# Decoder layer on one core: scores of two key tiles in a row, weighted sums two tiles at a time

## The reference

```
Q = split_heads(layernorm(x) @ Wq + bq)         # 4 batches, 16 heads, 256 queries, 8
K, V = split_heads(ctx @ Wk + bk), split_heads(ctx @ Wv + bv)   # 1601 keys
attn = softmax(Q @ K.T / sqrt(8))
x = x + merge_heads(attn @ V) @ Wo + bo
x = x + ffn(layernorm(x))
```

## Time and profile before

| | |
|---|---|
| median of 3 runs | 417.07 us (414.47 to 417.73) |
| the profiled execution's own time | 413.62 us |
| its span, first to last instruction | 411.8 us |
| busy: PE, DVE, ACT, POOL | 357.9, 306.6, 299.4, 131.6 us |
| mean granted clock of PE | 0.925 of full speed |

### The profile page before, as it was taken

How to read it: one execution, slowest core, us unless ns; L and a number is a source line. 1 busy time by engine, 2 the same in 40 slices (tenths; PEclk the granted TensorE clock), 3 DMA queues, 4 the chain that set the end, 5 groups by cost and what they waited for, 6 DMA issues and landing times.

```text
span 411.8 us, 11548 instructions
## 1 busy us (share of the span) xinstructions
PE 357.9 (87%) x4598; PEld 164.8 (40%) x4598; DVE 306.6 (74%) x692; ACT 299.4 (73%) x637; POOL 131.6 (32%) x205
## 2 busy tenths in 40 slices
PE   1645988989989989999898999998989999798946
PEld 0332333444534444444344444444334344353334
DVE  2373998779889988798788887998778899690022
ACT  1321226888979799889697898897697998969921
POOL 5721000379120206897200137992000036000010
PEclk9966555999999999999999999999899999999968
DMA  7063370003507312235160331343211420000000
GB/s 294 12 240 122 139 249 40 2 27 130 173 27 169 123 38 60 93 130 163 35 173 14 107 96 53 121 136 96 80 40 47 130 61 21 2 15 2 2 0 15
DMA packets 22203, 35.77 MB, mean 87 GB/s; under 512 B 1604, under 2 KB 19694, under 8 KB 22150
## 3 DMA queue, kind: packets, MB, share of 16 engines
q1 hardware_dynamic: 22150, 35.05, 26.8%
HBM read 19.25 MB, written 11.96 MB: 76 GB/s over the span
## 4 chain that ended last, share of the span: by engine, by line
PE 47%; DMA 13%; POOL 12%; ACT 11%; DVE 7%; issue 5%; SPq 4%; POOLq 0%; ACTq 0%; DVEq 0%
PE wsum L1013 16%; PE score L1027 10%; PE ring L983 8%; PE ring L1047 8%; DMA q_rows<-q_parts 5%; ACT probs L873 5%; POOL k_parts L547 4%; DMA k_rows<-k_parts 4%; POOL k_rest L584 3%; POOL k_parts L589 3%; DVE part_max L690 2%; DMA k_unit<-k_rows 2%; DMA q_unit<-consts 1%; SPq L435 1%; POOL xn L600 1%
## 5 line engine op out<-in xcount | busy, mean ns | idle before, releaser
L690 DVE TENSOR_REDUCE part_max<-ring 128x1 f32<-128x401 f32 x512 | 261.0, 568 | 43.8 <-PE ring L1047 42.8
L873 ACT ACTIVATE probs<-score 128x512 f32<-128x512 f32 (+1 forms) x416 | 223.1, 597 | 41.6 <-PE score L1027 38.1
L1047 PE MATMUL ring<-k_unit,q_unit 51*128 51x401 bf16 x512 | 143.2, 355 | 9.9 <-DMA q_unit<-consts 5.1
L1013 PE MATMUL wsum<-probs,v_unit 128*32 128x256 f32 (+1 forms) x1664 | 135.7, 394 | 2.0 <-ACT unit_ctx L878 2.0
L1027 PE MATMUL score<-q_unit,k_unit 51*128 51x256 bf16 (+1 forms) x832 | 123.9, 278 | 7.3 <-ACT probs L873 5.0
L1027 PEld LDWEIGHTS score<-q_unit,k_unit 51*128 51x128 bf16 (+1 forms) x832 | 47.2, 97 | 100.6 <-ACT probs L873 60.9
L1047 PEld LDWEIGHTS ring<-k_unit,q_unit 51*128 51x128 bf16 x512 | 47.3, 95 | 30.1 <-DVE part_max L690 10.8
L1013 PEld LDWEIGHTS wsum<-probs,v_unit 128*32 128x32 f32 (+1 forms) x1664 | 39.7, 109 | 41.3 <-issue 24.6
L547 POOL TENSOR_TENSOR max_parts<-neg_max,c_sb 128x8 bf16<-128x8 f32 x16 | 3.4, 210 | 150.8 <-DVE neg_max L694 150.7
L621 POOL TENSOR_SCALAR prob_norm<-prob_self,prob_rsum 128x128 f32<-128x128 f32 (+1 forms) x12 | 9.0, 766 | 43.1 <-DVE prob_rsum L766 43.1
L927 ACT ACTIVATE v_aug<-ring 128x128 f32<-128x128 f32 (+1 forms) x60 | 10.5, 261 | 16.1 <-PE ring L983 16.1
(11 more groups left out here) (111 smaller groups left out, 290.3 us busy)
## 6 DMA issues: line engine op xcount, KB each, us to landing
k_unit<-k_rows SPq DMA_DIRECT2D x32, 300.2 KB
v_unit<-v_aug SPq DMA_DIRECT2D x16, 234.0 KB, 5.9
ctx_sb<-ctx_t SPq DMA_DIRECT2D x4, 800.5 KB, 7.4
k_rows<-k_parts SPq DMA_DIRECT2D x4, 601.5 KB, 3.2
k_rows<-k_parts SPq DMA_DIRECT2D x4, 599.2 KB, 3.4
k_rows<-k_parts SPq DMA_DIRECT2D x4, 401.0 KB, 4.1
k_rows<-k_parts SPq DMA_DIRECT2D x4, 399.5 KB, 4.1
even<-ffn_rows SPq DMA_DIRECT2D x3, 512.0 KB, 3.8
```

Of the source, the lines that this page charges most:

```text
L690: v_.tensor_reduce(part_max[:, par, q, head, hp, c:c + 1], ring[s][:, 0:CW], AX.X, ALU.max)\
L873: a_.activation(probs[0:rows, i % PB, :], score[i % EB][0:rows, :], ACT.Exp)\
L1013: last = mm(wsum[32 * j:32 * j + 32, 0:S], v_unit[0:rows, u, VQ * t + VW * j:VQ * t + VW * j + 32], probs[0:rows, i % PB, S * (j // 2):S * ...
L1047: mm(ring[s][:, 0:CW], q_unit[rows, u, hp, P * q:P * (q + 1)], k_unit[rows, u, L * hp + (CW - 1) * c:L * hp + (CW - 1) * c + CW], start=Tr ...
```

## The change

In a tile of even number g the side work is held back and no PV is issued; the tile of odd number then brings its scores and maxima, the held and its own side work, and two PVs in a row, those of tiles g - 4 and g - 3. The even tile's side work is not held if it is one of the three long feed-forward steps (h0, h1, out) or if the tile is a unit's last. The same instructions are issued as before, with the same buffers.

```diff
+LONG = ("h0", "h1", "out")
 ...
+    held = []
 ...
-        if t == 4 and v:
-            plan.append(("norm", v - 1))
+        side = [("norm", v - 1)] if t == 4 and v else []
         if t == TURN_AT[u] and v + 1 < UNITS:
-            plan.append(("mT", v + 1))
-        for *what, off in (SIDE if b < B - 1 else SIDE_LAST).get((u, t), []):
-            if 0 <= b + off < B:
-                plan.append((*what, b + off))
-        if t >= 3:
-            plan.append(("PV", v, t - 3))
-        elif v:
-            plan.append(("PV", v - 1, KT - 3 + t))
-    assert not todo
+            side.append(("mT", v + 1))
+        side += [(*what, b + off) for *what, off in (SIDE if b < B - 1 else SIDE_LAST).get((u, t), []) if 0 <= b + off < B]
+        g = KT * v + t
+        if g % 2 == 0 and t < KT - 1 and not any(item[1] in LONG for item in side):
+            held = side
+            continue
+        plan += held + side
+        held = []
+        if g % 2:
+            plan += [("PV", *divmod(i, KT)) for i in (g - 4, g - 3) if i >= 0]
+    assert not todo and not held
     return plan
```

## The result

The changed kernel takes 439.35 us, the median of four runs (438.80 to 446.77), against 415.77 us (414.30 to 417.73) for the kernel before in runs on the same chip: ratio 1.056, 95% interval 1.049 to 1.063. The forecast was 432 us, range 418 to 446, slower with a chance of 0.78. Sign and mechanism held; the size was 7 us short, and of the difference itself 15.7 us were worked out and 23.6 measured. The time lies just above the band of 423 to 439 that had most of the chance. Some executions run in a slower state with a lower granted clock (446.77 us here, at 0.900 against 0.922 to 0.926); ratios and intervals leave them out, medians hold all.

What follows compares the result with a forecast made beforehand. PE was taken to set the pace, with PE, ACT and DVE balanced within a tenth. 7.8 + 2.3 + 4.2 + 7.7 - 3.2 - 6.1 - 1 + 4 = +15.7 us gave 432.8 against the median, stated as 432, range 418 to 446.

Steps and rivals of the forecast that it cites:

- The third free score buffer: In a joined pair the fourth score waits for the first exp: bare pair 2.46 us against 2.13, +0.33.
- pairs of scores alone: Six pairs without maxima in units 14 and 15 go from 2.02 to about 2.40 us: +2.3 us in all.
- Old waits absorb 3.6 us: In 39 pairs with hardly a wait, existing waits take 3.6 us off floors of 11.4, leaving +7.8 us.
- Six maxima +0.30: In 7 pairs with six maxima, the sixth waits for a ring slot: 2.76 us against 2.46, 2.1 us in all.
- mT: At the ends of units 1, 5, 9 and 13, PE waits for ACT's copies behind four exps: +4.2 us.
- Copy of wsum, even units: In 7 even units the next PV waits for ACT's copy behind four exps: +1.1 us each, +7.7 us.
- Copy of wsum, odd units: In 8 odd units the copy hides under a run of scores and a 0.4 us wait goes: -3.2 us.
- The waits for q_unit absorb 6.1: Transfer waits in tiles 2.7, 6.7 and 10.7 hide what PE loses in the two units before: -6.1 us.
- "Behind" +4: ACT and DVE late at a pair's start make the new waits longer than their floors: +4 us, bounds 0 and 26.
- Rival 3: ACT starves in each pair, and late ACT delays the fourth score again: +26 to +34 us, 440 to 450; chance 0.21.
- rival 1: The drain counts and waits close up, 0.25 us saved a pair: 402 to 412 us; chance 0.09.
- the other 0.11: Per pair, the 0.20 us before PV goes and the next score comes 0.09 behind the last: 0.11 us saved.

Runs made afterwards that it cites:

- The short exp: Each exp on 256 of its 512 columns: the changed kernel took 421.94 us (1.012), the kernel before with the same edit 405.56 us (0.972).
- the fourth buffer: Four score buffers in place of three, ring of three in place of four: changed kernel 466.08 us (1.119), kernel before 433.84 us (1.041).
- holding alone: The kernel before with side work held as in the change, but a PV behind each tile, three tiles behind: 424.74 us (1.016).
- mT not held: The changed kernel, but an even tile that carries mT (units 1, 5, 9, 13) holds nothing: 439.34 us (1.055).
- nothing held: The changed kernel with side work behind its own tile, PVs still two at a time: 430.2 us (1.031).
- the shorter maxima: The changed kernel with DVE's maxima reading 200 of 401 columns: 433.57 us (1.033).
- three profiles whose copies have cover: Changed kernel with odd units' last PV one pair earlier: 429.64 us; also with mT in even tiles holding nothing: 429.55; or no side work held: 423.61.

## Why the prediction was right, and where it was short

- **The third free score buffer: right, to 0.01 us.** 2.46 us was worked out from four rows, and all bare pairs have it; the 21 pairs of this kind, side work or not, grew together by the +6.9 that was said. The short exp (+0.12) and the fourth buffer (no difference left without maxima) show the cause. Five of the six pairs of scores alone became 2.46 too, not 2.40; the sixth, which carries mT, 2.65.
- **Old waits absorb 3.6 us: wrong, 0.** I took waits of 0.1 us in pairs "nearly without waits" for something that a new wait could hide. Where in the pair they stood I had not looked; that they stood elsewhere than the new wait is likely, but not shown.
- **Six maxima +0.30: too small, +0.47 on average.** The step forgot that the side work takes a ring slot as well, and so waits for one more drain. Where no side work stood behind them (13.5), it was +0.30 exactly.
- **mT: right in kind, 3.7 for 4.2.** The experiment adds what the working did not see: with the copies early, half of the loss is held by the ring.
- **Copy of wsum, even units: right,** 7.6 for 7.7, and the cheapest to mend.
- **Copy of wsum, odd units: the step that failed.** I took 0.4 us from tile 4.3, which is an even unit, and multiplied by eight. The page had the bound: PE waited 2.0 us for unit_ctx in all fifteen boundaries, and of the eight odd units only units 3, 13 and 15 waited at all (0.19, 0.19 and 0.47). And these pairs are joined like all others, so they pay for the run as well: +1.5 in place of -3.2, 4.7 us of the 10 that were missing. Tile 3.3 before, then the same pair of the changed kernel, where the wait for the copy has gone and one for an exp and one for a ring slot have come (3.51 us before, 3.89 with the change):

```profile
131.56 0.64 PE L1013 MATMUL wsum<-probs,v_unit 128*32 128x256 f32 x8 [0.19 <-ACT unit_ctx L878]
...
135.08 0.28 PE L1033 MATMUL score<-q_unit,k_unit 51*128 51x256 bf16 x1 [0.19 <-ACT probs L879]
...
136.01 0.41 PE L1072 MATMUL ring<-c_sb,unit_ctx 128*128 128x128 f32 x2 [0.23 <-DVE part_max L696]
```

- **The waits for q_unit absorb 6.1: right in sum (5.7),** but only for what PE loses after the chain has begun. From tile 5.1 to 6.6 the changed kernel falls back by another 4.7 us (from 9.1 to 13.8 behind the old one), and that is what the wait of 2.1 hides, beside the 1.1 of cover that holding moves behind it. With holding alone PE lost 0.8 there, and the waits grew.
- **"Behind" +4: the number came out (3.7), the content did not.** It was meant for ACT and DVE late at a pair's start. 3.3 of it is the clock in units 4 and 8, behind a wait that I had priced, and of a fall of the clock the sum had nothing. As some executions with the same wait have no such fall, the agreement is luck.
- Rival 3 lay nearest in time (440 to 450), but not in kind: ACT's lateness doesn't build up, the bare pair is the same 2.46 everywhere and shrinks with the exp, and DVE's load could be cut by 100 us without touching it. Of rival 1's saving of 0.25 a pair the 0.14 between two PVs is in the rows and is outweighed; the other 0.11 no run shows by itself.

Left open: what decides whether the clock falls behind a wait of this size.

## What to carry to other kernels

When instructions are put into longer runs to save changes of mode, count the buffers that the run fills and the ring slots that it takes, side work included: a run of four outputs over three buffers waits for its own first consumer, however idle that consumer is, and the working from four timeline rows gives the price to a hundredth. A wait that is to vanish is worth at most what the page puts down for it in all places together; look there before multiplying one row by a count. And ask of each small copy between two neighbours in the order what ACT has ahead of it: seven such places were worth 8 to 10 us here, with what the clock gave back, about as much as the third buffer in pairs with at most four maxima (6.9 + 2.6).

## What was not expected of the hardware

- One wait of 0.9 us of PE can cost more by the clock than by itself: with PE busy 2.30 of 3.54 us, the granted clock went from 1.00 to 0.50 behind it for about 10 us in unit 4, 1.75 us lost in the next pair alone. The same wait in unit 12 left the clock at 1.00 in one profile and was followed by 0.66 in another. Four profiles have this wait in units 4, 8 and 12, and the clock fell behind it in two of three places (the change), three (mT not held), one (nothing held) and none (the shorter maxima); in the three profiles whose copies have cover it fell in none of these units. That suggests that the wait has a part in it; what else decides is open. The kernel before has one such fall too, 3.4 us long from 289.0 us on, behind the wait of 2.57 us for q_unit.
- A third PV in a row costs the same 0.43 us as a second: (1.50 - 0.64) / 2.
- The stretch before tile 0.0, the same program in eleven of the profiled kernels, took between 59.8 and 61.7 us: differences in span of 2 us are not all in the part that was changed.
